# Two weight rings, a quantising multiply and cast on ScalarE, six masked rows on GpSimd, and a new order

## The reference, cut to what matters

```python
# layer 0, feed-forward: 2 of 8 experts for each row
h = jax.nn.silu(x @ Wg[i]) * (x @ Wu[i]);  output = output + w_i * (h @ Wd[i])
# layer 1, attention: scores below the 54th largest of a row are cut
thr = jax.lax.top_k(scores, 54)[0][..., -1:]
scores = jnp.where(scores < thr, -jnp.inf, scores)
out = jnp.einsum('bsn,bnd->bsd', jax.nn.softmax(scores), V) @ W_o.T
# layer 1, feed-forward: inputs of both matrices rounded to 8 bits, row by row
scale = 127.0 / jnp.clip(jnp.max(jnp.abs(x), axis=-1, keepdims=True), EPS, None)
xq = jnp.clip(jnp.round(x * scale), -128.0, 127.0) / scale
```

## Time and profile before

| | us |
|---|---|
| median of 3 runs (453.79 to 455.31) | 454.04 |
| the profiled execution, whole | 452.51 |
| its span in the trace | 450.8 |
| DVE, PE, ACT, POOL busy in it | 306.5, 359.8, 172.7, 48.8 |

### The profile page before, as it was taken

The page is one execution under the profiler, slowest core; times in us unless marked ns, Lnnn a source line. Parts: engine busy times, 40 slices in busy tenths (PEclk is TensorE's granted clock), DMA queues, the critical chain, the costliest instruction groups (busy, mean ns, idle before and its releaser), DMA issues.

```text
span 450.8 us, 6595 instructions
## 1 busy us (share of the span) xinstructions
PE 359.8 (80%) x2077; PEld 287.6 (64%) x2082; DVE 306.5 (68%) x776; ACT 172.7 (38%) x294; POOL 48.8 (11%) x100
## 2 busy tenths in 40 slices
PE   0999999997999986399998789579958446567975
...
DVE  2623474643201341063999999999999999999994
...
GB/s 249 173 310 98 310 224 296 84 103 358 37 281 211 236 229 316 245 224 96 321 258 293 191 231 159 133 107 123 125 68 54 0 0 153 45 142 140 82 15 58
DMA packets 70809, 76.38 MB, mean 169 GB/s; under 512 B 5356, under 2 KB 69496, under 8 KB 70776
## 3 DMA queue, kind: packets, MB, share of 16 engines
...
...
## 4 chain that ended last, share of the span: by engine, by line
PE 36%; DVE 33%; issue 12%; DMA 9%; POOL 4%; ACT 4%; SPq 1%; ACTq 1%; POOLq 0%; DVEq 0%
PE S L826 11%; PE GU L904 8%; DVE fold L1190 7%; DVE cand_h L1178 7%; PE A L853 5%; PE O L913 4%; DVE cand_l L1185 4%; DMA xg<-xs 3%; DVE fold L1195 3%; DVE row L1218 3%; DMA xs<-xn,idx_u 2%; POOL xs L544 2%; DMA x_res<-x 2%; PE T L840 2%; DVE gabs L1296 2%
## 5 line engine op out<-in xcount | busy, mean ns | idle before, releaser
L904 PE MATMUL GU<-xgT,ew_ring 128*128 128x128 f32 x480 | 60.9, 281 | 9.1 <-issue 8.1
L857 PE MATMUL A<-pT,v_sb 128*128 128x128 f32 (+1 forms) x416 | 59.3, 304 | 10.2 <-ACT pT L608 5.8
L904 PEld LDWEIGHTS GU<-xgT,ew_ring 128*128 128x128 f32 x480 | 58.1, 196 | 13.7 <-issue 9.1
L857 PEld LDWEIGHTS A<-pT,v_sb 128*128 128x128 f32 (+1 forms) x416 | 56.9, 218 | 13.5 <-issue 7.6
L608 ACT ACTIVATE pT<-T 128x512 f32<-128x512 f32 x64 | 31.8, 514 | 87.6 <-PE T L840 85.7
L840 PE MATMUL T<-ident,row 128*128 128x128 f32 (+1 forms) x208 | 34.9, 302 | 32.3 <-DVE row L1218 27.0
L1178 DVE MAX8 cand_h<-fold 128x8 f32<-128x801 f32 x56 | 54.7, 985 | 0.1
L840 PEld LDWEIGHTS T<-ident,row 128*128 128x128 f32 (+1 forms) x208 | 27.6, 156 | 40.5 <-issue 31.0
L853 PE MATMUL A<-v_sb,pT 128*128 128x256 f32 (+1 forms) x208 | 50.7, 388 | 0.0
L826 PE MATMUL S<-k_sb,xT 128*128 128x400 f32 (+2 forms) x128 | 49.0, 516 | 1.3 <-ACT xT L593 1.1
L826 PE MATMUL S<-k_sb,qT 128*128 128x400 f32 (+2 forms) x128 | 45.8, 503 | 2.6 <-ACT qT L665 2.1
...
## 6 DMA issues: line engine op xcount, KB each, us to landing
...
xg<-xs ACTq DMA_DIRECT2D x30, 128.0 KB, 3.6
ys<-y_sb ACTq DMA_DIRECT2D x30, 128.0 KB, 3.3
...
```

The source lines that it names most:

```text
L857: mm = pe.matmul(A_bank[:, o * P:(o + 1) * P], v[0:r, a, o * P:(o + 1) * P], pT[0:r, j, a, :], start=m == 0 and o == 0, stop=m == NMC - 1 ...
L904: mm = pe.matmul(gu_bank(*key)[:, a * F + f * P:a * F + (f + 1) * P], ew_ring[:, w % NW, a, k, f * P:(f + 1) * P], cols[:, k, :], start=k ...
```

## The change

1. `ew_ring` (3 slots of three matrices) becomes `wg_ring` (3 slots of Wg and Wu) and `wd_ring` (3 slots of Wd), the same memory in all. The step `wl` becomes `wg` and `wd`. GU waits for two loads and `wg` reuses a slot behind the GU three tiles earlier; `down` waits for its own load.
2. `xmul` and `q4e` are issued by ACT instead of DVE.
3. For tiles 0 to 5 the step `cut` is gone. In its place POOL makes, in four column units each, `ge` (comparison with the threshold, in place in `row3`) and `cutp` (times the exponentials), and ACT sums the row in a copy with an accumulator (`psum`). pT.3.t.u waits for `cutp` of its own unit, rc3.t and pairH and pairL of t+2 wait for `psum`. Tiles 6 and 7 are cut by DVE as before.
4. ORDER is new throughout; some waits are written for any order of the chunks of a row. The rings of V are written in another form, with the same two slots in use.

```diff
-                elif op == "wl":
+                elif op in ("wg", "wd"):
                     g, j = key
...
+                        if i >= NWG:
+                            sp.wait_ge(GU_done, n("GU", *WG_BY[i - NWG][1:]))
+                        for a, w in enumerate((Wg, Wu)):
...
+                        if i >= NWD:
+                            sp.wait_ge(down_done, n("down", *WD_BY[i - NWD][1:]))
...
+                elif op == "ge":
+                    t, u = key
+                    m0, m1 = 4 * P * u, min(M, 4 * P * u + 4 * P)
+                    pool.wait_ge(thr_done, n("thr", t))
+                    pool.wait_ge(exp3_done, n("exp3", t))
+                    pool.tensor_scalar(p_row(t)[:, m0:m1], row3[:, t % 4, m0:m1], thr3[:, t:t + 1], None, ALU.is_ge) \
+                        .then_inc(ge_done, 1)
+                elif op == "cutp":
...
+                    pool.wait_ge(ge_done, n("ge", t, u))
...
+                    pool.tensor_tensor(p_row(t)[:, m0:m1], p_row(t)[:, m0:m1], e_row(t)[:, m0:m1], ALU.mult) \
+                        .then_inc(cutp_done, 1)
...
+                elif op == "psum":
+                    t = key[0]
+                    act.wait_ge(cutp_done, n("cutp", t, NU - 1))
+                    act.activation(e_row(t)[:, 0:M], p_row(t)[:, 0:M], ACT.Copy, accum_out=sum3[:, t, 0:1]) \
+                       .then_inc(psum_done, 1)
...
+                    act.activation(xn4[:, t % 2, :], xn4[:, t % 2, :], ACT.Copy, bias=MAGIC, scale=xscl[:, t:t + 1]) \
+                       .then_inc(xmul_done, 1)
...
+                    act.activation(xqT[:, t % 2, :, :].rearrange("p k s -> p (k s)"),
+                                   t_bank("q4", t)[:, :].bitcast(I16)[:, 0:D], ACT.Copy).then_inc(q4e_done, 1)
```

More of the change, by code:

```diff
@@ L71 @@
[L71 to L95, removed]
@@ L126 @@
-yst.1.12 mul.1.13 pT.3.1.3 maxL.2.2 pvm.3.1.0 pTe.3.1.2 pairL.3 repL.2.2 GU.1.14 ldv.3.1.2 pTe.3.1.3 ldv.3.1.3
-maxH.2.6 maxL.3.0 pvm.3.1.1 silu.1.14 mul.1.14 repL.3.0 ldv.3.2.0 pvm.3.1.2 x3.0 maxL.3.1 maxL.2.3 down.1.13 ldv.3.2.1
-repL.3.1 pvm.3.1.3 ye.1.13 st4.0 yst.1.13 aTe.1 down.1.14 ag4.0 maxL.3.2 cent.0 ye.1.14 pairH.3 yst.1.14 wo.1 merge.2
-va4.0 thr.2 xabs.0 rs4.0 exp3.2 maxH.3.0 xmx.0 repL.3.2 gat.5.1 xdeq.0 x3.1 gat.5.0 maxL.3.3 gat.4.0 st4.1 xinv.0
-repH.3.0 gat.4.1 ag4.1 cut.2.0 upd.5.0 pT.3.2.0 cent.1 rc3.2 va4.1 upd.5.1 rs4.1 pT.3.2.1 xscl.0 xabs.1 pTe.3.2.0
@@ L161 @@
[L161 to L165 removed]
+ldx.0 mask.0 ldk.1.0.0 ldx.2 ldk.1.0.1 ldk.1.0.2 ldx.1 ldk.1.0.3 ldx.3 stats.1.2 aggr.1.2 stats.1.0 aggr.1.0 var.1.0
@@ new lines @@
+yst.1.13 ldv.3.1.2 down.1.14 cutp.1.2 repH.2.3 pTe.3.1.1 maxH.2.4 ye.1.14 ldv.3.1.3 yst.1.14 wo.0 repH.2.4 cutp.1.3
+pT.3.1.2 maxH.2.5 psum.1 pT.3.1.3 pvm.3.1.1 repH.2.5 gat.5.0 pTe.3.1.2 maxH.2.6 gat.5.1 pTe.3.1.3 ldv.3.2.0 pvm.3.1.2
+pairH.3 gat.4.1 merge.2 thr.2 pairL.3 exp3.2 pvm.3.1.3 ldv.3.2.1 gat.6.0 maxL.3.0 repL.3.0 upd.5.0 aTe.1 ge.2.0 x3.0
+maxL.3.1 wo.1 maxH.3.0 st4.0 gat.7.0 upd.6.0 repL.3.1 cutp.2.0 maxL.3.2 ag4.0 nmax.3 upd.5.1 va4.0 cent.0 xabs.0 rc3.1
+x3.1 rs4.0 pT.3.2.0 upd.7.0 gat.4.0 xmx.0 xdeq.0 xinv.0 xscl.0 st4.1 xmul.0 ag4.1 pTe.3.2.0 va4.1 repH.3.0 q4.0 ge.2.1
```

300 lines of the change are left out of this document (182 added, 118 removed).

## The result

| | before | after |
|---|---|---|
| median of 4 runs each on one chip | 453.92 us | 464.23 us (462.29 to 467.75) |
| ratio, 95% interval | | 1.0234 (1.0175 to 1.0293) |
| profiled execution, its span | 452.51, 450.8 | 464.89, 463.1 |
| up to the first fold | 210.2 | 211.3 |
| first fold to the last threshold | 206.1 | 220.7 |

The changed kernel is slower by 2.3%, where 1.8% faster was forecast. The three marks say where: the first piece is 1.2 us longer, the tail 3.5 us shorter, as forecast, and the middle piece 14.6 us longer, where 3.5 us shorter was forecast (6.0 less 2.5 of stalls).

What follows compares the result with a forecast made beforehand. DVE bounds stage 3, with PE and scatter latency before it and a chain through all engines after. 450.8 - 1.4 - 6.0 - 3.5 + 2.5 = 442.4 us of span, 445.6 us as median; range 439 to 454.

Steps and rivals of the forecast that it cites:

- The three marks: Where the forecast split the time: first fold at 210.16 us, last threshold at 416.27, tile 7's residual at 433.18.
- the first piece: Start to first fold, set by PE's work and two scatters' latency: 1.4 us earlier, ends 5 early and 3 late.
- the tail: Last threshold to end, a chain through all engines: 3.5 us shorter, 31.0 against 34.5, ends 1 and 5.
- the middle piece: First fold to last threshold, where DVE is full: 6.0 us shorter before 2.5 us of stalls.
- what `rank.0` was to gain by going first: In the first piece: `rank.0` ahead of s1 and pT steps, worth 4.9 us of PE.
- The price of overlap: In the middle piece: 6.3 us of summed DVE durations saved, scaled by 206.1 over 216.8 to 6.0 us.
- The stalls: Waits for GpSimd rows and at PE's pT.3: spares seemed enough; 2.5 us charged in all, ends 0 and 8.
- rival 1: GpSimd and DVE block each other on SBUF, slowing folds and upd: 6 us, total 451.6; chance 0.17.
- the work pulled forward: Stage 4 steps (gabs, cent, xabs, fin, small ones) moved ahead of the last threshold: 7.4 us more for DVE there.
- GpSimd's prices: Masking for 512 columns: `ge` 0.85 us, `cutp` 1.34; a row 9.5 us including seven gaps of 0.30.
- Rival 2: GpSimd is slow and DVE waits once a tile; decides from a row of about 18 us; 465 us at 2.5 times; chance 0.10.
- rival 4: The order doesn't meet the chip: PE waits at pT.3, GU behind, then DVE; 8 us idle, 454 us; chance 0.08.

Runs made afterwards that it cites:

- a_vlate: The changed kernel with only the V load ldv.3.1.0 moved behind the weight load wg.1.13 in SP's queue; 455.4 us, ratio 1.0081 to before.
- a_inter: The changed kernel with DVE's chain steps interleaved, leaving 41 instead of 81 neighbours that depend on each other; 460.0 us, ratio 1.0195 to before.
- c_both: The changed kernel with the V load behind wg.1.13 and DVE's chains interleaved (41 instead of 81 dependent neighbours); 456.6 us, ratio 1.0066 to before.
- v_dvecut: The changed kernel with the V load behind wg.1.13 and the cuts of all rows back on DVE; 462.5 us, ratio 1.0253 to before.
- d_late: The changed kernel with the V load behind wg.1.13 and DVE's chains interleaved only from thr.0 on; 454.8 us, ratio 0.9979 to before.
- e_mix: The c_both kernel with the cut of row 0 alone back on DVE, right behind thr.0; 464.7 us, ratio 1.0154 to before.
- d_noxq: The changed kernel with the V load behind wg.1.13 and `xmul` and `q4e` back on DVE; 462.0 us, ratio 1.0116 to before.
- b_adj: The kernel before with only 51 MAX8 moved right ahead of the MATCH_REPLACE8 that needs each; 463.1 us, ratio 1.0249 to before.
- b_all: All code changes (two weight rings, `xmul` and `q4e` on ACT, cuts on GpSimd) in the order of the kernel before; 507.5 us, ratio 1.1215 to before.
- b_xq: The kernel before, old order, with the two weight rings and `xmul` and `q4e` on ACT, cuts on DVE; 452.4 us, ratio 1.0004 to before.

## Why the prediction was wrong

**Up to the first fold: forecast 1.4 us earlier, 1.2 us later in the profile.** The single steps missed. The start lost what was forecast: the first `stats` stands at 8.50 instead of 6.63. But xgT.0.0 came at 113.10 (forecast 110.4, has 113.32): the scatter began at 95.21, 0.9 us earlier than before instead of 2.9, so most of what `rank.0` was to gain by going first isn't there; where it went isn't shown. Group 0 then gained 4.1 us (forecast 1 less 0.6), with xgT.1.0 at 183.53 against 187.89 in the earlier trace rows, but s3.0.0 stood 21.7 us behind it instead of 17.9. PE was busy 19.1 of these 21.7 us (14.9 of 16.2 before) at a mean granted clock of 0.77 (0.87 before), and a `down` waited 1.93 us for y_sb. In the eight profiles with the new order and this start (after, a_vlate, a_inter, c_both, v_dvecut, d_late, e_mix, d_noxq) the first fold lies between 206.4 and 212.7 us, in five with the old order and cuts on DVE between 206.4 and 210.2; the 2.5 us between forecast and result are less than that spread, and neither gain nor loss of this piece is shown.

**First fold to last threshold: forecast 202.6 us, measured 220.7.** All of the error is here, in three steps.
1. *The price of overlap.* The prediction summed durations to 216.8 us, saw that before needed 206.1 and applied this ratio to the new order. But the ratio changes with the order: a MAX8 or MATCH_REPLACE8 overlaps with the step behind only where that step doesn't need it. Added up over the trace before, DVE's instructions between the marks last 227.4 us and 23.2 us of it overlap, 12.1 behind MAX8 and MATCH_REPLACE8 and 11.1 behind the other steps; after it is 16.8 us, 7.0 and 9.8. With 76 long spacings the new order loses 8.1 us (62 x 0.13); the sums of the trace have it as 5.1 us of overlap that is gone and 3.1 us of gaps of under 0.06 us each. b_adj shows the price with the order alone changed, and d_late shows part of it won back.
2. *The stalls.* The prediction went through the spares of DVE, PE and POOL and charged 2.5 us. It didn't walk SP's list, although the weights' steps and the V loads both changed places in it. 5.9 us, shown by a_vlate; other stalls than this one hardly came, so the term was 3.4 us too small.
3. *Contention,* rival 1, which the forecast put at nothing. The rival came, with 4.1 us by v_dvecut where it had said 6. The signs that it named are there, folds above 0.98 us and upd above 0.48. The single cases are as large as one POOL instruction:
```profile
294.68 1.80 DVE L1214 SCALAR_TENSOR_TENSOR x_res<-yg,w_top,x_res 128x256 f32<-128x256 f32 x1
...
387.38 1.74 DVE L1247 TENSOR_TENSOR fold<-row 128x801 f32<-128x801 f32 x1
```
The Trainium skill (SBUF — State Buffer, Who interferes with whom) has it that a VectorE instruction with two SBUF inputs contends with GpSimd's reads and one with a single input doesn't, unless it runs in a mode that uses both ports. The trace agrees: these two were stretched, and on the larger halves the 15 MAX8 beside GpSimd's masking took 989 ns and the 41 others 991. Of the single-input steps cent was stretched, 0.49 us at most instead of 0.35, and once 1.19 us in b_all; whether it ran in such a mode no view says. GpSimd is held up too: its one product of 65 columns beside the fold at 387.38 took 1.08 us, the other five 0.32.

3.4 + 8.1 + 4.1 = 15.6 us of the 18.1 us between forecast and result. The last 2.5 us are not assigned to a run; the trace has 1.3 us less overlap behind the other steps, and the work pulled forward, priced at 7.4 us, adds up to 8.1 in v_dvecut against b_xq.

**Last threshold to the end: forecast 31.0, measured 31.0,** as 16.3 + 14.7 where 15.4 + 15.6 was said; that the two misses cancel is luck. And the reason given for the tail, that less work is left in it, was priced as if it were free. v_dvecut against b_xq shows the trade: 7.4 us (8.1 by the trace) of steps pulled forward into a stretch in which DVE is full, for 3.0 us in the tail. And `xmul` and `q4e` on ACT, counted with the gains, bring nothing that the runs can tell in the old order and nothing in the tail of the new one.

**GpSimd's prices.** `cutp` was right to 5%. `ge` was taken from a select of one input with an affine index, as the nearest row; it took 1.59 us instead of 0.85. Even so a row took 9.2 to 9.9 us from its first `ge` to its last `cutp` (24.0 for row 2, with gathers in between), where 9.5 was forecast. This is luck: the 0.30 us between POOL's instructions, 2.1 us a row, isn't there, and made up for `ge`. Rival 2 (a slow GpSimd) decides from 18 us on, and no fold waited for a psum. It was closer than forecast all the same: psum.0 began at 253.9, 5.9 us behind the last product, and ended 2.3 us ahead of pairH.2, where 6.3 us were forecast.

**Rivals.** Two came together. The first is answered above. The fourth, that the order doesn't meet the chip, named PE at pT.3, GU behind it and DVE behind that; GU and DVE did wait, at 262.85 to 269.62, but it was SP that began it and the weights that were late. Its price was 8 us in idle time of DVE, and the one block cost 5.9. What no rival held is the dependent neighbours, the largest item. The range ended at 454, where the fast end of rival 4 lay, and the chance of slower, 0.15, was mostly on a slow GpSimd.

What was right in it: that DVE counts between the two marks, the length of the tail, `cutp`, and that no fold would wait for POOL. The offload as such gains what it should: 11.4 us of cuts less 4.1 of contention is 7.3, measured 7.7 in the order made for it. It can't be had in the old order as it stands, and the new one costs 11.
